# Band products of one tile in every pair, and row maxima turned in the third and sixth pair

## The reference

```python
scores = jnp.einsum('bhid,bhjd->bhij', qh, kh)
rel = jnp.clip(pos[None, :] - pos[:, None], -K, K) + K        # K = 64
bias_r = jnp.einsum('bhid,rd->bhir', qh, rel_pe)
bias = jnp.take_along_axis(bias_r, rel, axis=-1)
attn = jax.nn.softmax(scores + bias, axis=-1)
out = jnp.einsum('bhij,bhjd->bhid', attn, vh)
```

## Time and profile before

| | before |
|---|---|
| median of 3 runs | 2521.58 us |
| lowest and highest | 2520.6 and 2535.18 us |
| profiled execution | 2522.68 us |
| its span, first to last instruction | 2521.0 us |
| PE, ACT, DVE, POOL busy in the span | 90%, 66%, 69%, 25% |
| granted TensorE clock, mean | 0.973 |

### The profile page before, as it was taken

The page is one execution under the profiler, slowest core; times in us unless marked ns, Lnnn a source line. Parts: engine busy times, 40 slices in busy tenths (PEclk is TensorE's granted clock), DMA queues, the critical chain, the costliest instruction groups (busy, mean ns, idle before and its releaser), DMA issues. The chain is left out here.

```text
span 2521.0 us, 46743 instructions
## 1 busy us (share of the span) xinstructions
PE 2256.5 (90%) x14642; PEld 1243.9 (49%) x14642; DVE 1737.7 (69%) x3444; ACT 1660.6 (66%) x1983; POOL 628.0 (25%) x1117
## 2 busy tenths in 40 slices
PE   4996579999999999999999999999999999699997
PEld 3564234444444444444444444444444444488886
DVE  2443457777777777777777777777777775488885
ACT  2432157777777777777777777777777777466676
POOL 0001111122111221212212122221222210466673
PEclk9999579999999999999999999999999999899999
DMA  6997767777767777777777777777777762333321
GB/s 193 364 341 276 183 175 192 192 199 202 194 190 195 197 202 193 195 194 197 201 191 196 195 197 198 195 197 194 191 202 196 197 191 76 108 96 108 109 78 43
DMA packets 452027, 468.57 MB, mean 186 GB/s; under 512 B 106901, under 2 KB 410726, under 8 KB 451942
## 3 DMA queue, kind: packets, MB, share of 16 engines
q1 hardware_dynamic: 355830, 368.91, 49.9%
q0 software_dynamic: 83072, 89.92, 15.1%
q10 hardware_dynamic: 13040, 8.80, 1.1%
HBM read 244.73 MB, written 221.25 MB: 185 GB/s over the span
## 5 line engine op out<-in xcount | busy, mean ns | idle before, releaser
L890 ACT ACTIVATE probs<-weigh_ps 128x1024 f32<-128x1024 f32 x1024 | 1047.4, 1023 | 377.0 <-PE weigh_ps L1058 375.6
L1018 PE MATMUL ring_ps<-keys,queries 48*128 48x512 f32 x2048 | 832.6, 463 | 28.7 <-DVE partial_max L931 18.7
L942 DVE CUSTOM_DVE_ANT_1 ring_ps<-ring_ps,band_all 128x512 f32<-128x512 f32 x1008 | 680.7, 715 | 229.8 <-PE ring_ps L1018 229.5
L931 DVE TENSOR_REDUCE partial_max<-ring_ps 128x2 f32<-128x1024 f32 x512 | 627.7, 1226 | 285.5 <-PE ring_ps L1018 240.7
L1058 PE MATMUL weigh_ps<-queries,keys 50*128 50x512 f32 (+3 forms) x2688 | 735.4, 379 | 0.9 <-ACT probs L890 0.5
L1075 PE MATMUL sum_ps<-probs,values 128*32 128x512 f32 x4096 | 547.5, 606 | 0.1
L1018 PEld LDWEIGHTS ring_ps<-keys,queries 48*128 48x128 f32 x2048 | 363.9, 187 | 353.3 <-issue 170.9
L1043 PE MATMUL weigh_ps<-ident,band_all 128*128 128x128 f32 x2048 | 362.6, 290 | 126.1 <-ACT carried L878 113.1
L878 ACT ACTIVATE carried<-weigh_ps 128x1024 f32<-128x1024 f32 x256 | 261.9, 1024 | 190.2 <-PE weigh_ps L1006 167.3
L1043 PEld LDWEIGHTS weigh_ps<-ident,band_all 128*128 128x128 f32 x2048 | 216.9, 141 | 325.2 <-ACT carried L878 189.2
L1058 PEld LDWEIGHTS weigh_ps<-queries,keys 50*128 50x128 f32 x2688 | 358.3, 186 | 17.0 <-ACT probs L890 8.9
(11 more groups left out here) (113 smaller groups left out, 1744.7 us busy)
## 6 DMA issues: line engine op xcount, KB each, us to landing
band_scr<-carried SPq DMA_DIRECT2D x256, 512.0 KB, 5.1
band_all<-band_scr SPq DMA_DIRECT2D x128, 512.0 KB, 4.4
band_all<-band_scr SPq DMA_DIRECT2D x128, 256.0 KB, 3.3
keys<-k_scr POOLq DMA_DIRECT2D x128, 240.0 KB, 8.5
k_scr<-k_parts SPq DMA_DIRECT2D x16, 1792.0 KB, 8.4
q_scr<-q_parts SPq DMA_DIRECT2D x16, 1024.0 KB, 6.3
queries<-q_scr POOLq DMA_DIRECT2D x128, 128.0 KB, 3.1
o_scr<-weighted_s SPq DMA_DIRECT2D x64, 256.0 KB, 5.8
```

What stands on the lines that cost most here:

```text
L890: nc.scalar.activation(probs[:, u % PROBS], weigh_ps[weigh_of["scores", at]][:], ACT.Exp).then_inc(s_pr, 1)
L931: nc.vector.reduce_max(partial_max[:, g, :, e, 0], ring_ps[:, first:second + 1], AX_X).then_inc(s_seen, HG)
L942: nc.vector.tensor_tensor_reduce(out=both, in0=both, in1=bias, scale=1.0, scalar=LOWEST, op0=ALU.add, op1=ALU.max, accum_out=partial_max[: ...
L1018: nc.tensor.matmul(dst, query_rows(c, h, ROWS, tile * P, (tile + 1) * P), key_rows(c, h, ROWS, c0, c0 + 512), start=True, stop=True, tile_ ...
```

## The change

Seven edits belong together.

1. `bands_at` and `band_index` count tiles instead of pairs of tiles: each of the eight pairs makes the band product of one tile (two matmuls of 256 columns) into the first half of each bank of a score buffer.
2. In the pair's order on PE, the band product stands ahead of `lagging` instead of behind it.
3. `copy_band` copies 128 x 512 instead of 128 x 1024, eight times a step instead of four. It waits for a free `band_out` slot only at even tiles.
4. Every pair has three uses of the score buffers, so the two exponentials of a pair always have the same buffer and the band the other.
5. SP still moves the same 512 KB pieces, now at units 3, 7, 11 and 15: first the read of the previous piece, then the write of this one.
6. The turns stand at units 4 and 10 (third and sixth pair), and SP issues their transfers at the same units, first in its order.
7. Which of a unit's two looks goes first (`look_heads`) follows the turns.

```diff
--- before.py
+++ after.py
@@ -616,20 +616,20 @@
             def looks_at(step, u):
                 return 0 <= step * UNITS + u + LOOK_AHEAD < G * UNITS
 
-            TURN_AT = {8: 0, 12: 1}
+            TURN_AT = {4: 0, 10: 1}
 
             def turns_at(step, u):
                 return u in TURN_AT and 0 <= step + 1 < G
 
             def bands_at(step, m):
 
-                return m >= QT and 0 <= step + BAND_STEPS < G
+                return 0 <= band_index(step, m) < G * NT
 
             def look_index(step, u):
                 return step * UNITS + u + LOOK_AHEAD
 
             def band_index(step, m):
-                return (step + BAND_STEPS) * NM + m - QT
+                return (step + BAND_STEPS) * NT + m - QT
 
             def turn_index(step, u):
                 return 2 * (step + 1) + TURN_AT[u]
@@ -663,7 +663,7 @@
                             occupy(("turn", turn_index(step, u)), 1)
                         if looks_at(step, u):
                             n = look_index(step, u)
-                            look_heads[n] = (1, 0) if m % 2 == 0 and u % 2 == 0 and not turns_at(step, u) else (0, 1)
+                            look_heads[n] = (1, 0) if u % 2 == 0 and (m % 2 == 0) != turns_at(step, u) else (0, 1)
                             slots = LOOK_SLOTS[m % 2][u % 2]
                             for h in look_heads[n]:
                                 occupy(("look", HG * n + h), slots[h])
@@ -673,8 +673,7 @@
                         if filled:
                             weigh_of[what], weigh_before[what] = weighs % 2, in_weigh[weighs % 2]
                             in_weigh[weighs % 2] = what
-                        if what[0] == "scores" or m >= QT:
-                            weighs += 1
+                        weighs += 1
 
             def cnt(i, per_step, value):
 
@@ -716,7 +715,7 @@
                 def write_bands(i, n):
 
                     c, m = n // NM, n % NM
-                    sp.wait_ge(s_be, cnt(i, NM, n + 1))
+                    sp.wait_ge(s_be, cnt(i, NT, 2 * n + 2))
                     sp.dma_start(flat(band_scr, band_base(c, m), [[BAND_ROW, P], [P * BAND_ROW, HG * 2], [1, 2 * P]]),
                                  band_out[:, n % BANDS_OUT].rearrange("p h e c -> p (h e) c")
                                  ).then_inc(s_bw[n % BANDS_OUT], 16)
@@ -760,18 +759,16 @@
 
                 def unit(i, step, u):
                     m = u // 2
+                    if turns_at(step, u):
+                        load_minus_max(i, step, TURN_AT[u])
                     if u == 5 and step > 0:
                         store_sums(i, step - 1)
-                    if u == 9 and turns_at(step, 8):
-                        load_minus_max(i, step, 0)
-                    if u == 13 and turns_at(step, 12):
-                        load_minus_max(i, step, 1)
-                    if u == 0 and bands_at(step - 1, NT - 1):
-                        read_bands(i, band_index(step - 1, NT - 1))
-                    if u % 2 and bands_at(step, m):
-                        if bands_at(step, m - 1):
-                            read_bands(i, band_index(step, m - 1))
-                        write_bands(i, band_index(step, m))
+                    if u % 4 == 3:
+                        chunk = band_index(step, m) // 2
+                        if 0 <= chunk - 1 < G * NM:
+                            read_bands(i, chunk - 1)
+                        if 0 <= chunk < G * NM:
+                            write_bands(i, chunk)
 
                 sp.wait_ge(s_set, 5)
                 for h in range(HG):
@@ -872,11 +869,12 @@
                     nc.scalar.activation(weighted_s[:, c % 2], sum_ps[:], ACT.Copy).then_inc(s_ws, 1)
 
                 def copy_band(i, n):
-                    act.wait_ge(s_bp, cnt(i, NM, n + 1))
-                    if n >= BANDS_OUT:
-                        act.wait_ge(s_bw[n % BANDS_OUT], cnt(i, 16 * NM // BANDS_OUT, 16 * (n // BANDS_OUT)))
-                    nc.scalar.activation(band_out[:, n % BANDS_OUT].rearrange("p h e c -> p h (e c)"),
-                                         weigh_ps[weigh_of["band", n]][:], ACT.Copy).then_inc(s_be, 1)
+                    chunk, e = n // 2, n % 2
+                    act.wait_ge(s_bp, cnt(i, NT, n + 1))
+                    if e == 0 and chunk >= BANDS_OUT:
+                        act.wait_ge(s_bw[chunk % BANDS_OUT], cnt(i, 16 * NM // BANDS_OUT, 16 * (chunk // BANDS_OUT)))
+                    nc.scalar.activation(band_out[:, chunk % BANDS_OUT, :, e], weigh_ps[weigh_of["band", n]][:, :, 0:2 * P],
+                                         ACT.Copy).then_inc(s_be, 1)
 
                 def copy_turned(i, n):
                     act.wait_ge(s_turn, cnt(i, 2, n + 1))
@@ -982,7 +980,7 @@
                         elif kind == "scores":
                             pe.wait_ge(s_pr, cnt(i, UNITS, n + 1))
                         else:
-                            pe.wait_ge(s_be, cnt(i, NM, n + 1))
+                            pe.wait_ge(s_be, cnt(i, NT, n + 1))
 
                 def seen_count(n):
 
@@ -993,19 +991,17 @@
                     return ring_ps[:, slot_of[what]]
 
                 def band_product(i, n):
-                    c, m = n // NM, n % NM
-                    if m == 0:
+                    c, tile = n // NT, n % NT
+                    if tile == 0:
                         pe.wait_ge(s_q[c % SLOTS], i * (16 * LOADS) + 16 * LOADS * (c // SLOTS + 1))
                     wait_for(i, weigh_before["band", n])
                     dst = weigh_ps[weigh_of["band", n]]
-                    for e in range(2):
-                        tile = 2 * m + e
-                        for h in range(HG):
-                            table = rel_terms[h * ROW_TILE:h * ROW_TILE + ROWS, :].rearrange("p (a c) -> p a c", a=3)
-                            moving = table[:, 0:3:2] if tile == NT - 1 else table[:, 0:2]
-                            last = nc.tensor.matmul(dst[:, h, e * 2 * P:(e + 1) * 2 * P].rearrange("p (a c) -> p a c", a=2),
-                                                    query_rows(c, h, ROWS, tile * P, (tile + 1) * P), moving,
-                                                    start=True, stop=True, tile_position=(h * ROW_TILE, 0))
+                    for h in range(HG):
+                        table = rel_terms[h * ROW_TILE:h * ROW_TILE + ROWS, :].rearrange("p (a c) -> p a c", a=3)
+                        moving = table[:, 0:3:2] if tile == NT - 1 else table[:, 0:2]
+                        last = nc.tensor.matmul(dst[:, h, 0:2 * P].rearrange("p (a c) -> p a c", a=2),
+                                                query_rows(c, h, ROWS, tile * P, (tile + 1) * P), moving,
+                                                start=True, stop=True, tile_position=(h * ROW_TILE, 0))
                     last.then_inc(s_bp, 1)
 
                 def look(i, n, h):
@@ -1103,9 +1099,9 @@
                     if step >= 0:
                         turn_bands(i, step, m, 0)
                     products(i, step, m, 0)
-                    lagging(i, step, m)
                     if bands_at(step, m):
                         band_product(i, band_index(step, m))
+                    lagging(i, step, m)
                     if step >= 0:
                         turn_bands(i, step, m, 1)
                     products(i, step, m, 1)
```

## The result

| | before | after |
|---|---|---|
| median | 2521.09 us (4 runs) | 2567.3 us (4 runs) |
| lowest and highest | 2520.32 and 2535.18 | 2560.36 and 2591.65 |
| ratio to before, 95% interval | | 1.0189 [1.0124, 1.0254] |
| profiled execution, its span | 2522.68, 2521.0 | 2563.75, 2562.1 |
| mean granted clock | 0.973 | 0.948 |

The account below looks back on a forecast made before the run. PE's instructions plus its wait for ACT's band copy were taken as the bound. Terms summed to -1.63 us a step, 99 us over 61 steps, plus 8 at the start, minus 2 at the end: 2417 us, range 2385 to 2455.

Parts of the forecast that it names:

- SyncE: SP's queue: reads 7 us behind writes against 5.1 of landing, last read some 15 us ahead of DVE's need; covered, no cost.
- a stalled DVE would stall PE one to one: Remark on SP's band reads: without the cover, time that DVE stalls would stall PE equally; no cost was counted.
- C: Rival on ACT: the 512-element copy takes 1.02 us, so pairs start late; step 29.2 us, 2547 us; chance 0.05.
- A: Rival on PE: half a band product costs a whole one, 1.36 us a step; step 28.1, about 2480 us; chance 0.11.
- the 0.25 that the prediction had named as a sign of being wrong: On PE: the prediction is wrong if the band product's two matmuls take over 0.25 us to what follows.
- The waits that go: PE's four waits per step for ACT's band copy, at the starts of pairs, go: -2.19 us a step.
- The same band products in smaller pieces: On PE: eight products of two matmuls at 0.17 us replace four at 0.34; 0 us a step, bounds nothing and +1.36.
- the ties between PE, ACT and DVE: Near-equal finish times: shared exponential buffer +0.10, band product behind previous exponential +0.20, DVE's reduction +0.10 us a step.
- The second pair: ACT copies the sums before the band, so PE waits in the third pair: +0.56 us a step, bounds 0.3 and 0.9.
- Start: First step with scores: earlier turns and transfers remove most of PE's waits for the maxima, 8 of 12.5 us.

Follow-up runs that it names:

- write_first: The changed kernel with SP issuing the write of each band piece before the read of the piece before it; 2431.33 us, ratio to before 0.9648.

## Why the prediction was wrong, by its own steps

**The step that failed is "SyncE".** It said that reads stand 7 us behind writes against 5.1 us of landing, that DVE's need is 15 us away, and that this was covered several times over. The two landing times are right as medians of before. What the step left out is that the program's order on the queue makes a read that waits hold up the writes behind it. The question was not how long a piece has, but how much of each step SP is taken: 26.4 of 28.7 us. The median of 5.1 us hid the writes that take 8 to 10, and the new places in the step made more of them. The 4.4 us failed in the same way: the one transfer that DVE waited for took 8.0 on average at its new place. What the runs showed in place of cover is a queue with 8.8 us of slack in 1200, DVE and behind it PE standing in 23 of 60 steps, and 133 us lost. Both the exchange of write and read and the small loads take all of it away. I asked who waits for whom on PE's side and never on SP's.

**The remark that a stalled DVE would stall PE one to one** was right in kind and too small in size: PE stood 2.8 us in a stalled step on average and then ran at the lower clock, and the step lost about 6.

**The rivals** all sat on PE and ACT. None was on the queue that the change reordered. C, the slower one, put its mechanism in the copy, which measured 592 ns on average, near the 0.60 us of the earlier trace rows. (In its sum, 29.9 without the last 0.8 is 29.1, not 29.2.) A's condition did come true: two matmuls cost nearly what four had cost, 0.31 against 0.34 us, and that is over the 0.25 that the prediction had named as a sign of being wrong. A's price did not: its step was 28.1 us, and the undisturbed one is 27.4.

**The rest can be read in write_first**, where the chain is out of the way:

- *The waits that go*, 2.19 us a step: right. One of four is left, in the third pair, as said.
- *The same band products in smaller pieces*, forecast at 0.17 each: mis-sized. In the kernel after, the weighted block follows the product's start by 0.31 us on average. That is 8 x 0.14 = 1.1 us a step more than counted, while the step is only 0.3 longer than forecast. That a part fell into the ties between PE, ACT and DVE, and that the rest is the reason for 27.4 instead of 27.1 us, is likely but not shown.
- *The second pair*, 0.56: it showed 0.39 as idle time, and its removal gave 0.31.
- *Start*, 8 us: more came. The first copy of the weighted sums comes at 352.6 us in the kernel after and at 351.7 in write_first, where it came at 366.5, and neither waits for the maxima at the first step with scores.
- Together, the forecast of 2417 without the failed step compares with 2431 for write_first. That it is this near owes something to luck, since the products were too cheap, and the second pair and the start erred the other way.

## What to carry to other kernels

Before a change that makes the bounding engine faster, ask for the waits of every queue that must keep its pace, the DMA-issuing ones too. The time for which a queue waits for its producers is its slack, and the time for which it waits for its own transfers is not. Where one queue both writes and reads back, issue the next write ahead of the read that has to wait; two exchanged lines turned 1.9% slower into 3.5% faster here. Moving transfers within a step changes what they meet, so the landing time of the old places does not carry over. And a list of waits can hide short ones: before calling a wait gone, compare the start of the waiting instruction with the end of what it waits for.

## What the runs showed of the hardware

After a stall of 2.35 us in a stretch of full activity, TensorE's granted clock was 0.57 on average from 1026 to 1030 us, so for most of it at the lower level. The kernel with 23 stalled steps lost 133 us, of which 67 were PE's waits behind DVE. From 400 to 2200 us the granted clock stood at its lower level for 143 us in all, which at half the speed is up to 72 us lost, and that fits the rest. Landings of the same 512 KB writes ranged from under 4 to over 10 us at a DMA share of 0.68 to 0.74, and were 6.4 us on average against 3.5 with the loads of keys and values made small. The traffic then was 176 GB/s, against 205 in write_first at the same pace of steps.
